# A four-layer network in one program: every engine loop's head at slot 0 of a fetch block, its closing branch announced each turn

## The reference

```python
h = _layernorm(x) * (1 + ca) + sa
x = x + ga * attn(h)
h = _layernorm(x) * (1 + cb) + sb
x = x + gb * ffn(h)
```

```python
x = attn_layer(shift_tokens(x), Wqkv[i], q_scale[i], k_scale[i], Wo[i]) + x
x = ffn_layer(shift_tokens(x), ln_g[i], ln_b[i], W1[i], b1[i], W2[i], b2[i]) + x
```

## Time and profile before

| What | us |
|---|---|
| runs of the kernel before, median (3 runs) | 5669.87 |
| the profiled execution | 5680.2 |
| its span, first to last instruction | 5678.5 |
| PE busy in the span | 5099.3 (90%) |
| DVE busy | 3936.6 (69%) |
| ACT busy | 3359.2 (59%) |
| POOL busy | 2606.4 (46%) |

### The profile page before, as it was taken

The page is one execution under the profiler, slowest core; times in us unless marked ns, Lnnn a source line. Parts: engine busy times, 40 slices in busy tenths (PEclk is TensorE's granted clock), DMA queues, the critical chain, the costliest instruction groups (busy, mean ns, idle before and its releaser), DMA issues. The chain is left out here.

```text
span 5678.5 us, 131658 instructions
## 1 busy us (share of the span) xinstructions
PE 5099.3 (90%) x50825; PEld 3440.8 (61%) x50825; DVE 3936.6 (69%) x6558; ACT 3359.2 (59%) x5891; POOL 2606.4 (46%) x1596
## 2 busy tenths in 40 slices
PE   7999855799799999999999999999999999799897
PEld 4455422465477767776777677767776666566544
DVE  4888789677477767776777677767776666567553
ACT  4555422355476766766667667667666666555434
POOL 2555411000255555565566566656665555366300
PEclk8999866799899999999999999999999999999898
DMA  2111100000000010001000100010001000000020
GB/s 61 60 60 60 34 0 0 7 2 2 28 12 14 11 29 14 11 11 30 14 11 11 32 11 11 11 32 11 11 11 32 12 12 9 17 2 2 23 60 19
DMA packets 75570, 113.62 MB, mean 20 GB/s; under 512 B 21888, under 2 KB 52816, under 8 KB 71440
## 3 DMA queue, kind: packets, MB, share of 16 engines
q1 hardware_dynamic: 67040, 109.78, 7.1%
q10 hardware_dynamic: 8256, 0.03, 0.1%
HBM read 69.56 MB, written 2.49 MB: 13 GB/s over the span
## 5 line engine op out<-in xcount | busy, mean ns | idle before, releaser
L2193 POOL TENSOR_TENSOR lt_qk<-lt_qk,lt_rot 128x1024 f32<-128x1024 f32 x384 | 908.0, 2365 | 234.8 <-DVE lt_rot L2556 234.8
L2203 POOL TENSOR_TENSOR lt_prob<-lt_prob,lt_total 128x1024 f32<-128x1024 f32 x192 | 365.4, 1903 | 1100.0 <-DVE lt_total L2578 1100.0
L2240 PE MATMUL lt_ps<-lt_w_qk,lt_xs 128*128 128x512 f32 x1536 | 754.3, 615 | 46.3 <-issue 31.9
L2198 POOL TENSOR_TENSOR lt_qk<-lt_qk,lt_rnorm 128x1024 f32<-128x1024 f32 x384 | 727.2, 1905 | 114.8 <-ACT lt_rnorm L2432 107.2
L2291 PE MATMUL lt_ps<-lt_z,lt_fold 128*128 128x256 f32 x3072 | 678.8, 379 | 1.2 <-ACT lt_z L2460 1.2
L2291 PEld LDWEIGHTS lt_ps<-lt_z,lt_fold 128*128 128x128 f32 x3072 | 583.6, 190 | 121.4 <-ACT lt_z L2460 24.3
L2553 DVE TENSOR_TENSOR lt_qk<-lt_ps,lt_table 128x1024 f32<-128x1024 f32 x384 | 468.4, 1220 | 107.8 <-ACT lt_sq L2422 99.2
L2568 DVE TENSOR_REDUCE lt_nmax<-lt_ps 128x16 f32<-128x1024 f32 x192 | 229.9, 1197 | 379.4 <-PE lt_ps L2259 379.4
L2556 DVE TENSOR_TENSOR lt_rot<-lt_ps,lt_table 128x512 f32<-128x512 f32 x768 | 490.8, 681 | 0.0
L2563 DVE TENSOR_REDUCE lt_norm<-lt_sq 128x16 f32<-128x1024 f32 x384 | 464.0, 1208 | 0.0
L2240 PEld LDWEIGHTS lt_ps<-lt_w_qk,lt_xs 128*128 128x128 f32 x1536 | 275.0, 195 | 278.3 <-issue 273.3
(11 more groups left out here) (400 smaller groups left out, 10142.4 us busy)
## 6 DMA issues: line engine op xcount, KB each, us to landing
mb_bs<-mb_rows SPq DMA_DIRECT2D x16, 1536.0 KB, 7.6
lt_xw<-lt_xw SPq DMA_DIRECT2D x192, 128.0 KB, 2.3
mb_bs<-mb_rows SPq DMA_DIRECT2D x16, 512.0 KB, 4.2
mo_gate_b<-mo_rows SPq DMA_DIRECT2D x16, 512.0 KB, 5.7
lt_xs<-h SPq DMA_DIRECT2D x96, 64.0 KB, 1.9
lt_w_qk<-in_L_ffn_Wqkv SPq DMA_DIRECT2D x6, 1024.0 KB, 5.2
lt_xs<-h SPq DMA_DIRECT2D x96, 63.8 KB, 1.9
lt_wvT<-in_L_wvT SPq DMA_DIRECT2D x6, 512.0 KB, 7.3
```

The source lines that it names most:

```text
L2193: pool.tensor_tensor(qk[:, u, :, :], qk[:, u, :, :], rot[:, u % 2, :, :], ALU.add).then_inc(sg["added"], 1)
L2198: pool.tensor_tensor(qk[:, u, :, :], qk[:, u, :, :], rnorm[:, u, :, :].to_broadcast([P, H, DH]), ALU.mult).then_inc(sg["qk"], 1)
L2240: last = pe.matmul(AT[u][:, 512 * k:512 * k + 512], xs[:, m.j, c:c + P], w_qk[:, a, 512 * k:512 * k + 512], start=True, stop=True)
```

## The change

```diff
+def engine_loop(eng, start, end):
+    return eng.bass.Fori(start, end, engines=bass.OrderedEngineSet([eng.engine]), hint_back_edge=True, head_slot={eng.engine: 0})
+
 def pairs(eng, count, body):
...
-        with eng.Fori(1, count // 2) as i:
+        with engine_loop(eng, 1, count // 2) as i:
             body(2 * i, 0)
             body(2 * i + 1, 1)
...
-        with eng.Fori(1, count) as n:
+        with engine_loop(eng, 1, count) as n:
             body(n, None)
...
-            with eng.Fori(2, B // 2) as i:
+            with engine_loop(eng, 2, B // 2) as i:
                 step(2 * i, 0)
                 step(2 * i + 1, 1)
...
             def layer(l, last):
-                with eng.Fori(0, B // 2 - 1) as i:
+                with engine_loop(eng, 0, B // 2 - 1) as i:
                     body(Item(l, 2 * i, 0), Item(l, 2 * i + 1, 1))
                     body(Item(l, 2 * i + 1, 1), Item(l, 2 * i + 2, 0))
...
-            with eng.Fori(0, L - 1) as l:
+            with engine_loop(eng, 0, L - 1) as l:
                 layer(l, False)
             layer(L - 1, True)
```

## The result

The changed kernel takes 5683.71 us in the median of 11 runs (5667.61 to 5692.44), the kernel before, run beside it, 5669.35 us (11 runs, 5666.11 to 5681.24). The medians differ by 14.4 us. The forecast was 5656, faster, with a range that ended at 5681.

What follows compares the result with a forecast made beforehand. TensorE, busy 90% of the span, was taken to bound the kernel, idling at missed code fetches. Terms of -29.2-5+15+0+1+3+1 = -14.2 us against 5669.87 gave 5656 us, range 5634 to 5681.

Steps and rivals of the forecast that it cites:

- (a): Last layer's loop at slot 0: seven blocks stay resident, three long turns become short, 29.2 us gone.
- (d): Outer loop's hint: could remove the outer miss, 16 us, but taken as overwritten by inner hints, 0.
- R1: Rival: the outer loop's hint works, header block and back edge come in time; 5640 us, chance 0.2.
- (e): Inner loops' hints, one instruction at each engine's head over 63 turns: +1 us, between 0 and +10.
- R3: Rival: hinted block takes its own line, middle layers' closing branches start to miss; about 5830 us, chance 0.04.
- R4: Rival: last loop's head misses slot 0 or seven blocks do not stay; 5690 us, chance 0.08.
- (g): Code behind the last loop shifts against block boundaries, a tiny burst may get a gap: +1 us (0 to +4).
- step (b): Last layer's first turn: slot 0 removes the gaps in bursts of tiny matmuls, -5 us (0 to -5.5).
- step (c): Nested inner head: second fetch behind outer edges and first entry, five at 3.0 us, +15 (0 to +22).
- the sign named for being wrong: Layer changes: the forecast is wrong if they cost over 5 us more each.
- step (f): Entries of all other loops: jumps over padding, next block already there on PE, +3 us (0 to +12).
- R2: Rival: padding at nested heads and other loop entries eats the gain; 5671 us, chance 0.18.

Runs made afterwards that it cites:

- e5: Changed kernel, but the inner loop of layers 1 to 4 keeps slot 0 without the hint; 5670.09 us, 0.9989 of the kernel before.
- e10: Kernel before, with only the last layer's inner loop on TensorE put at slot 150 with a hint; 5645.00 us, ratio 0.9954.
- e2: Kernel before, with every loop's head at slot 0 and no hints; 5673.40 us, ratio 1.0004.
- e8: Changed kernel, but slots and hints on TensorE only, other engines' loops as before; 5672.26 us, 0.9994 of the kernel before.
- e14: Changed kernel, but Mamba, fp4, causal and binary loops without slot or hint; 5679.38 us, 0.9999 of the kernel before.
- e1: Kernel before, with a hint on every loop and no slots; 5655.31 us, ratio 0.9964.
- e6: Kernel before, with the layer loop hinted on all engines and the last layer's inner loop on TensorE at slot 0, unhinted; 5633.64 us, ratio 0.9930.
- e7: Changed kernel, but the inner loop of layers 1 to 4 has neither slot nor hint; 5649.47 us, 0.9956 of the kernel before.
- e9: Kernel before, with only the last layer's inner loop on TensorE put at slot 150, unhinted; 5669.73 us, ratio 0.9994.
- e15: Kernel before, with the layer loop hinted on all engines and the last layer's inner loop on TensorE at slot 150, hinted; 5638.03 us, ratio 0.9928.

## Why the prediction was wrong

**Right.** (a): six equal turns, no q8 packet, branches under 250 ns. (d): the outer hint did nothing, and for the reason given: e5, in which the inner loop does not announce, has the branch at 0.46 us. R1 was a true mechanism with its condition unmet. (e): hints take 31 to 50 ns on PE, turns of the middle layers stay at 68.8 us. R3 and R4 did not occur. (g): 0.5 us behind the last layer.

**Right in size, not in its reason: step (b).** The first turn took 70.4 us for 75.3, with (a) 32.7 us against 34.2 forecast. But the gaps that slot 0 was to remove are there still (0.43 and 1.08 us), and the twin, free of them before, now has its own. What went was part of the idle time and the whole fall of the clock, 0.95 to 1.00; e10, at slot 150, has a gap of 1.59 us and a first turn of 69.9. That the -5 came out is luck.

**Mis-sized: step (c).** The second miss was there and of the forecast size: the idle time before L2246 behind the four outer branches is 8.28, 8.99, 8.38 and 8.40 us, where L2240 had 5.43, 5.94, 5.12 and 5.65, 12 us in all. What the step put at nothing is the rest of a layer change. The first turns behind it take 71.2 to 71.6 us in place of 69.3 to 70.0, 7 us in all, with the gaps in the bursts that moved code brings, and the code from the inner loop's exit to the outer branch takes 3 us more: 22.1 us in this trace, 5.5 a layer. In e2, e8 and e14, with PE's slots as here, it was 18 to 19 us, 4.5 to 4.7 a layer, so that the sign named for being wrong (over 5 us more per layer change) came true in this trace narrowly and in those not. The fifth entry, the first, was counted as 3 us; it cost 10.3: 7.5 of idle time, because the jump over the layer loop's own padding missed as well (4.04 + 3.20 us), and 2.8 in its first turn (71.6 us against 68.8 behind L2246).

**Failed: step (f), "On PE the next block is already there".** It was so at three of six forward jumps (last layer, causal, binary: 0.3 to 0.4 us), while those at Mamba, fp4 and the layer loop took 3.6 to 4.0 us. For the other engines I had the mechanism (a head further on is fetched on demand) and looked for it at the small loops and the last layer; the one place where the traces show a cost is the layer loop's entry, where ACT, DVE, POOL and SP each wait 2.7 to 3.5 us while PE waits too, 1.5 to 1.8 us of it on PE's path. The step's +3 stands against what is left of the +15.4 us ahead of the first closing branch when the 10.3 of the entry are taken off. Of these 5 us about 4 are the clock in Mamba's turns, 375.2 us for five in place of 371.2; e1 and e6 show 374.0 there and e2, e8 and e14 371.2 to 372.5, so that no edit is to blame for it. By the ratios the other engines are worth 14 us (e8) and the small loops about 11 (e14), the two overlapping, each to within 7 us.

**The sum.** With (c) at 22 + 10 and what lies ahead of the layers otherwise at about 5, in place of 15 and 3, the forecast's own sum is -14.2 + 17 + 2 = +5, which is what the traces show. R2, the padding eats the gain, is what happened, and its upper bounds were too low: 4.4 us for each of five entries, where a layer change cost 5.5 and the first entry 10.3. The remaining 6 us between the traces (+5.2) and the ratio (+11) are within what single executions differ by: runs of one kernel lie up to 25 us apart, and the profiled one of before 10 us above its median.

The Trainium skill's rule ("Advanced Engine Details and Errata", ISA Cache) that two lines are held is contradicted for TensorE once more: e10 runs a loop of eight blocks for six turns without a fetch.

**Not settled.** What sets every turn or every second one for eight unannounced blocks; why seven of the 35 first turns with moved code have no gap; what in the changed kernel costs 8 us more than in e2; why the jump at Mamba, 3.3 to 3.7 us in the five other traces with padding there, took 0.42 us in that of e7; the split of the small loops' cost between engines, and where most of the other engines' 14 us lies.

## What to carry to other kernels

Look for a loop whose closing branch misses, and treat that loop alone: here one head at a slot on one engine gave 0.52%, slots on every loop of every engine gave nothing (1.0004), and slots with announcements cost 0.19%. Padding ahead of a nested head puts two fetches in a row behind each outer back edge, and a hint in the inner loop takes the outer one's away: announce the outer loop if its branch misses and the inner one does not. Count every forward jump over padding as a possible miss, on every engine: on PE three of six missed.

## What the runs showed that I had not expected

- On PE a later announcement takes an earlier one's effect: the layer loop's branch took 0.46 us when its own came last (e5), 3.6 to 3.9 us when the inner loop announced after it.
- An announced closing branch keeps a body of eight blocks resident (e10, 559.0 us for the last layer) that without it misses (e9, 585.2 us). The layer loop's announcement makes the code behind that loop late (3.5 to 3.9 us at the next jump in e5, e6, e7 and e15, 0.4 without).
- A jump of ACT, DVE, POOL or SP to a block that is not there leaves a branch record of under 100 ns and a gap of 2.4 to 5.7 us behind it; on PE the branch record itself is long.
- A change on the other four engines alone altered how often PE's unchanged last loop missed (every turn for every second, 604.5 for 593.8 us).
